# A language-model block on one core: the linear scan cut into runs of four tokens instead of single steps

## The reference

```
h  = relu(causal depthwise conv of width 2 over fake_quant(emb)[ids])     # 8 x 512 x 128
u  = layernorm(h)
# linear recurrence, 4 heads of 64 states, the same A (64x64) for every head:
x_t = x_(t-1) A + u_t B            # x_0 = init_states; written in the reference as an
                                   # associative scan over complex logarithms
x  = exp(log x - max over the head's 64 states + 2)       # = e^2 * x / max|x|
h  = h + x C + u D
n  = layernorm(h);  x_attn = (n*g + b) attn_w^T + attn_b + n
out = h + gelu(gelu(x_attn fc1^T + b1) fc2^T next^T + ...)  # 8 experts by position, hidden size 512
```

## Time and profile before

| | |
|---|---|
| median of three runs | 188.50 us (188.31 to 188.63) |
| profiled execution: own time | 188.72 us |
| its span, first to last instruction | 186.9 us |
| granted TensorE clock, mean | 0.997 |
| busy: PE, PEld, DVE, ACT, POOL | 169.2, 154.3, 135.4, 108.6, 106.5 us |

### The profile page before, as it was taken

The page is one execution under the profiler, slowest core; times in us unless marked ns, Lnnn a source line. Parts: engine busy times, 40 slices in busy tenths (PEclk is TensorE's granted clock), DMA queues, the critical chain, the costliest instruction groups (busy, mean ns, idle before and its releaser), DMA issues.

```text
span 186.9 us, 3886 instructions
## 1 busy us (share of the span) xinstructions
PE 169.2 (91%) x1327; PEld 154.3 (83%) x1327; DVE 135.4 (72%) x410; ACT 108.6 (58%) x289; POOL 106.5 (57%) x173
## 2 busy tenths in 40 slices
PE   0598899999999999799898899999999999997993
PEld 0187779999989999688587899999999999986882
DVE  1868974775444446667988999988889898628883
ACT  3026997745443334543445496785949778595782
POOL 3107664699900000323979678397896969789600
PEclk9999999999999999999999999999999999999998
DMA  5994000000000000000000000001010100101003
GB/s 147 321 438 182 5 0 5 2 0 0 4 0 0 4 0 0 2 4 0 0 0 0 4 0 2 4 2 56 0 60 0 53 7 2 58 4 58 24 32 112
DMA packets 2327, 7.42 MB, mean 40 GB/s; under 512 B 254, under 2 KB 892, under 8 KB 2052
## 3 DMA queue, kind: packets, MB, share of 16 engines
q1 hardware_dynamic: 2162, 7.05, 10.0%
q10 hardware_dynamic: 146, 0.13, 0.2%
HBM read 5.09 MB, written 2.10 MB: 38 GB/s over the span
## 4 chain that ended last, share of the span: by engine, by line
PE 53%; POOL 14%; DVE 12%; issue 9%; ACT 8%; DMA 2%; ACTq 0%; POOLq 0%; DVEq 0%
PE bank L966 8%; PE bank L969 7%; PE bank L1106 6%; POOL hid_p L437 6%; PE bank L1126 5%; PE bank L994 5%; PE bank L1053 4%; POOL rstd L467 3%; PE bank L943 3%; PE bank L899 2%; PE bank L920 2%; PE bank L983 2%; PE bank L1050 2%; ACT gel L560 2%; POOL X L449 2%
## 5 line engine op out<-in xcount | busy, mean ns | idle before, releaser
L437 POOL TENSOR_TENSOR hid_p<-hid_f,hid_p 128x256 fp32r<-128x256 f32 x52 | 37.5, 741 | 14.5 <-ACT hid_p L602 12.6
L600 ACT ACTIVATE hid_f<-bank,pa 128x256 f32<-128x256 f32 x64 | 30.8, 485 | 12.7 <-PE bank L1106 12.5
L1106 PE MATMUL bank<-xaT_p,fc_p 128*128 128x256 f32 x192 | 35.4, 296 | 1.7 <-ACT corr L577 0.7
L1126 PE MATMUL bank<-hid_p,out_hi 128*128 128x256 f32 x128 | 32.0, 286 | 0.3 <-POOL hid_p L437 0.3
L509 ACT ACTIVATE X<-bank 128x128 f32<-128x128 f32 x64 | 17.6, 278 | 22.7 <-PE bank L969 22.5
L1106 PEld LDWEIGHTS bank<-xaT_p,fc_p 128*128 128x128 f32 x192 | 26.7, 189 | 4.7 <-ACT hid_p L602 1.7
L966 PE MATMUL bank<-uT,pa 128*128 128x128 f32 x128 | 25.2, 281 | 0.1
L1126 PEld LDWEIGHTS bank<-hid_p,out_hi 128*128 128x128 f32 x128 | 23.3, 188 | 1.0 <-POOL hid_p L437 0.6
L602 ACT ACTIVATE hid_p<-bank,pa 128x256 fp32r<-128x256 f32 x48 | 23.5, 489 | 0.0
L969 PE MATMUL bank<-X,pa 128*128 128x128 f32 x120 | 23.2, 275 | 0.0
L444 POOL TENSOR_TENSOR E<-E,corr 128x248 f32<-128x248 f32 (+4 forms) x5 | 3.1, 626 | 32.0 <-ACT corr L585 32.0
(11 more groups left out here) (126 smaller groups left out, 369.8 us busy)
## 6 DMA issues: line engine op xcount, KB each, us to landing
fc_w<-in_fc SPq DMA_DIRECT2D x2, 2048.0 KB, 12.1
out<-res SPq DMA_DIRECT2D x7, 256.0 KB, 2.0
pb<-in_pack_b SPq DMA_DIRECT2D x1, 320.0 KB, 4.1
pa<-in_pack_a SPq DMA_DIRECT2D x1, 279.0 KB, 3.0
out<-res SPq DMA_DIRECT2D x2, 128.0 KB, 1.7
pc<-in_pack_c ACTq DMA_DIRECT2D x1, 128.5 KB, 3.0
pw<-in_pack_a SPq DMA_DIRECT2D x1, 64.0 KB, 3.8
emb_w<-in_emb SPq DMA_DIRECT2D x1, 62.5 KB
```

The lines of the kernel that those rows point to most:

```text
L437: nc.gpsimd.tensor_tensor(hid_p[1][:, half, c, :], hid_f[:, m % HID_SLOTS, :], hid_p[0][:, half, c, :].bitcast(F32), ALU.subtract).then_in ...
L600: full = nc.scalar.activation(hid_f[:, m % HID_SLOTS, :], src, ACT.Gelu, bias=bias)
L1106: last = mm(bank[5 + n % 2][:, 0:HALF], fc1_p[w][:, e * HID + c * P:e * HID + (c + 1) * P], xaT_p[m][:, b % 2, half, :], start=(k == 0), s ...
L1126: last = mm(out_bank(b, half)[:, half * HALF:(half + 1) * HALF], out_p[w][:, e, c * CH:(c + 1) * CH], hid_p[m][:, half, c, :], start=(c == ...
```

## The change

Group by group, the scan is done in four runs of four tokens in each chunk, all runs at once.

- `run_piece(g, n)`: the state at the end of each run from zero, as four accumulating matmuls over 512 columns (4 batches x 4 runs x 32 chunks): token `q` of the run times B A^(3-q). 8 such matmuls a group; ACT copies 512 columns a half (`copy_runs`). The products B A, B A^2, B A^3 (`late_b`) are two new `prepare` tasks, B^T comes with the first input pack.
- `ends(g)`: three matmuls over 248 columns (A^12, A^8, A^4) and one DVE add make the chunk ends from the run ends; the five doubling steps are as before, but their adds are DVE's in both groups (`ks_add`). They work in place 0 of `X`, which has 17 places now (`E` and `corr` are gone).
- `last_step(g, r)`: four steps of 256 columns with A^4, one after the other, each with a DVE add, give the state after each run.
- `state_input`, `state_step`: the three tokens inside all runs, per half one matmul with B and one with A over 512 columns, copied by ACT (`copy_state`).
- The powers of A that are kept are 1, 2, 3, 4, 8, 12, 16. `prepare` has 18 tasks as before, with 23 instead of 26 blocks of 128 columns.
- Placement: group 0's runs stand in embedding rounds 6 and 7, `ends`, the first doubling step and `fuse(0)`, `fuse(1)` in rounds 8 and 9 (ACT makes the high part now). After them come group 0's carries, with the first half of group 1's runs and `fuse(2)`, `fuse(3)` between, then group 0's states. `attn_g` and `centre` move behind the first doubling add on DVE. The second half of group 1's runs, its carries and its states fill the rounds -3, -2 and -1 by the new `PLAN`, and `fc1_part(0, 0)` waits for the last of them.
- POOL has no part in the scan any more. The embedding's tiles keep their own memory.

```diff
+POWERS = (1, 2, 3, 4, 8, 12, 16)
+RUN = 4
+RUNS = T // RUN
...
-        X = sb("X", [P, NG, NP * GB, T, NCH])
-        corr = sb("corr", [P, CORR_SLOTS, NP * GB, NCH])
-        E = sb("E", [P, NG, NP * GB, NCH])
+        X = sb("X", [P, NG, NP * GB, EXT, NCH])
...
+        PLAN = {
+            -3: (("run", "run"), (), ("run", "run"), (), ("fuse", "carry"), ("fuse", "carry"), ("fuse", "carry"), (), ()),
+            -2: (("carry",), ("input",), ("fuse", "input"), ("carry",), (), ("carry",), ("carry",), (), ("carry",)),
+            -1: (("carry",), (), ("carry", "step"), ("input", "step"), ("input", "step"), ("input",), ("step",),
+                 ("input", "step"), ("step",))}
+        ORDER = (0, 1, MIXER, 2, 3, 4, 5, 6, 7)
...
+                def copy_state(g, n):
+                    q, a = divmod(n, NP)
+                    act.wait_ge(state_done[g], n + 1)
+                    nc.scalar.activation(every_run(g, a, q + 1), scan_bank(a).rearrange("p (b r k) -> p b r k", b=GB, k=NCH),
+                                         ACT.Copy).then_inc(x_ready[g], 1)
...
+                for n in range(1 + LEVELS + RUNS):
+                    if n == 2:
+                        dve.wait_ge(ld_pb, 16)
+                        dve.wait_ge(ld_pa, 32)
+                        nc.vector.tensor_scalar(attn_g[:], pb[:, PB["attn"]], pa[:, PA["ln_g"]], None,
+                                                ALU.mult).then_inc(attn_g_ready, 1)
+                        nc.vector.tensor_scalar(centre[:], ident, -1.0 / CH, None, ALU.add).then_inc(centre_ready, 1)
+                    carry_add(0, n)
+                    if n in (3, 4, 8, 9):
+                        fused_lo((3, 4, 8, 9).index(n))
...
                 def scan_part(j, places):
                     for n in places:
                         for what, i in scan_work(j, n):
+                            if what == "carry":
+                                carry_add(1, i)
+                        for what, i in scan_work(j, n):
                             if what == "fuse":
                                 fused_lo(i)
...
+                def run_piece(g, n):
+                    a, q = divmod(n, RUN)
+                    if n == 0:
                         pe.wait_ge(uT_ready, GB * (g + 1))
...
+                    last = mm(scan_bank(a), b_then(a, RUN - 1 - q), u_runs(g, q), start=(q == 0), stop=(q == RUN - 1))
+                    if q == RUN - 1:
+                        last.then_inc(run_done[g], 1)
+
+                def ends(g):
+                    pe.wait_ge(run_ready[g], NP)
...
+                    for r in range(RUNS - 1):
+                        last = mm(carry_bank(g, NCH - 1), power(T - RUN * (r + 1)), X[:, g, :, RUN * (r + 1), 0:NCH - 1],
+                                  start=(r == 0), stop=(r == RUNS - 2))
+                    last.then_inc(ends_done[g], 1)
...
+                def last_step(g, r):
+                    if r == 0:
                         pe.wait_ge(ks_ready[g], LEVELS)
...
+                    mm(carry_bank(g, NCH), power(RUN), X[:, g, :, RUN * r, :], start=True, stop=True).then_inc(last_done[g], 1)
...
+                def state_input(g, n):
+                    q, a = divmod(n, NP)
+                    if q >= 1:
+                        pe.wait_ge(x_ready[g], n - 1)
...
+                    mm(scan_bank(a), b_then(a, 0), u_runs(g, q), start=True, stop=False)
+
+                def state_step(g, n):
+                    q, a = divmod(n, NP)
+                    if n == 0:
+                        pe.wait_ge(last_ready[g], RUNS - 1)
+                    mm(scan_bank(a), a1, every_run(g, a, q), start=False, stop=True).then_inc(state_done[g], 1)
...
-                    for i in embed_round_steps(b):
-                        scan_step(0, i)
+                    if b in (NB - 2, NB - 1):
+                        for q in range(RUN):
+                            run_piece(0, (b - (NB - 2)) * RUN + q)
+                    if b >= NB:
+                        carry_step(0, b - NB)
+                        fuse(b - NB)
                 prepare(N_PREP - 1)
-                for lv in range(LEVELS):
-                    ks_step(0, lv)
-                    scan_step(1, lv)
-                for i in range(T):
-                    second_pass(0, i)
-                    if (i + 1) % (T // WITH_SECOND) == 0:
-                        scan_step(1, LEVELS + i // (T // WITH_SECOND))
+
+                for n in range(RUN):
+                    carry_step(0, n + 2)
+                    run_piece(1, n)
+                carry_step(0, 6)
+                fuse(2)
+                carry_step(0, 7)
+                fuse(3)
+                carry_step(0, 8)
+                state_input(0, 0)
+                state_input(0, 1)
+                state_step(0, 0)
+                carry_step(0, 9)
+                state_step(0, 1)
+                for n in range(NP, NP * (RUN - 1)):
+                    state_input(0, n)
+                    state_step(0, n)
...
                         pe.wait_ge(xaT_ready, b + 1)
                         if b == 0:
                             pe.wait_ge(fc1_split, NE)
-                            pe.wait_ge(corr_ready, T)
+                            pe.wait_ge(x_ready[1], NP * (RUN - 1))
+                            pe.wait_ge(last_ready[1], RUNS)
                             pe.wait_ge(fused_lo_ready, NE)
```

More of the change, by code:

```diff
@@ L294, in embed_round_steps @@
-        def embed_round_steps(b):
-            return range(sum(G0_STEPS[:b]), sum(G0_STEPS[:b + 1]))
+        FUSED_FRONT = 4
+        MIXER = 8
+        PLAN = {
[3 more added lines that the diff above has]
+                 ("input", "step"), ("step",))}
@@ L303, in numbered @@
         def numbered(plan):
-            done, out = dict(step=LEVELS + WITH_SECOND, doubling=0, fuse=FUSED_FRONT, second=0), []
-            for names in plan:
-                place = []
-                for name in names:
-                    place.append((name, done[name]))
-                    done[name] += 1
-                out.append(place)
-            assert done == dict(step=T, doubling=LEVELS, fuse=NE, second=T)
+            done, out = dict(fuse=FUSED_FRONT, run=RUN, carry=0, input=0, step=0), {}
+            for j, places in plan.items():
+                for n in ORDER:
+                    out[j, n] = []
+                    for name in places[n]:
+                        out[j, n].append((name, done[name]))
+                        done[name] += 1
+            assert done == dict(fuse=NE, run=NP * RUN, carry=1 + LEVELS + RUNS, input=NP * (RUN - 1), step=NP * (RUN - 1))
             return out
@@ L540, in _, with scan_copies @@
                         last.then_inc(u_act_ready, 1)
-                    for i in embed_round_steps(b):
-                        copy_step(0, i)
+                    if b in (NB - 2, NB - 1):
+                        copy_runs(0, b - (NB - 2))
+                    if b >= NB:
+                        copy_fused(b - NB)
                 copy_out_prep(N_PREP - 1)
-                for lv in range(LEVELS):
-                    copy_step(1, lv)
-                for i in range(LEVELS, LEVELS + WITH_SECOND):
-                    copy_step(1, i)
+                copy_runs(1, 0)
+                for e in range(2, FUSED_FRONT):
+                    copy_fused(e)
+                for n in range(NP * (RUN - 1)):
+                    copy_state(0, n)
+                def scan_copies(j, n):
+                    for what, i in scan_work(j, n):
+                        if what == "fuse":
+                            copy_fused(i)
+                        if what == "run" and i % RUN == RUN - 1:
+                            copy_runs(1, i // RUN)
+                        if what == "step":
+                            copy_state(1, i)
                 def gelu_out(j):
@@ L567, in _ @@
                         if j < 0:
[L568 to L586 removed]
+                            scan_copies(j, n)
                         if n == LAG - 1 and j >= 1:
@@ L608, in _ @@
                                                      bias=bias).then_inc(last_hi_act, 1)
+                        if n == 1 and j < 0:
+                            scan_copies(j, MIXER)
                         b = j + 1
@@ L829, in _ @@
                     if j < 0:
[L830 removed]
+                        scan_part(j, [2, 3])
                     high_parts(j, range(2, 4))
@@ L1137, in fill @@
                             else:
-                                {"step": scan_step, "doubling": ks_step, "second": second_pass}[what](1, i)
+                                {"run": run_piece, "carry": carry_step, "input": state_input, "step": state_step}[what](1, i)
                     else:
@@ L1153, in _ @@
                         mixer_out(mixed, 1)
+                    if j < 0:
+                        fill(j, MIXER)
                     if 0 <= attended < NB:
```

301 lines of the change are left out of this document (133 added, 168 removed).

## The result

The changed kernel takes 187.12 us (median of four, 187.07 to 187.26) against 188.47 for the kernel before; the ratio on record is 0.9937, with a 95% interval of 0.9923 to 0.995. Forecast were 186.0 with a range from 184.8 to 187.9. So the direction was right, and of the 2.5 us forecast 1.35 came by these two medians and 1.2 by the ratio. Its profiled execution took 187.07 us, with a span of 185.3. Run again with twelve executions, the same kernel gave 187.09 against 188.21, ratio 0.9946 (0.9928 to 0.9964). Ratios leave out executions in a slower state of the chip, of which there was one here (e6, 198.21 us at a mean clock of 0.854).

What follows compares the result with a forecast made beforehand. Scan PE-bound with group 0, then passed between PE and DVE, ACT, POOL. 31.1 + (62.7 - 2.65) + 8.8 = 100.0 at the first expert matmul; `transpose_xa(1)` 2.55 earlier; median 186.0 us, range 184.8 to 187.9.

Steps and rivals of the forecast that it cites:

- half-gain rival: Strided 512-column matmuls and copies cost their upper bounds, or prepare(17) waits 1.7: about 187.2 us, chance 0.20.
- hand schedule: New order laid out with trace prices, last gather at 31.1 to first expert matmul at 100.0, waits 8.8 us.
- `transpose_u(7)` waits behind `u`: Rounds 8 and 9: PE waits 0.5 us for DVE's last u, at 40.05, a wait hidden before.
- the first expert matmul behind an ACT copy: End of round -1: PE waits 0.85 us for the last state copy, first expert matmul at 100.0.
- after `attn(0)` PE waits 2.4: Round -2: the second last step's matmul waits 2.4 us, as DVE's add stands behind xh(1) until 82.8.
- the forecast's 153.3: Forecast time from the last gather's start to the end of the span: 184.4 - 31.1 us.
- ten waits: PE's waits from the last gather to the first expert matmul, summed as 8.8 us against 8.0 before.
- 1.5 for 40 matmuls at 0.04: Extra cost of strided 512-column matmuls at their upper bound, a ground for about 187.2 us, chance 0.20.
- The blocked adds: Group 0's carry adds on DVE slowed by POOL's split until 51.4: about 190.5 us, chance 0.11.
- POOL's adds were off every path: Rounds -2 to 0: removing POOL's second-pass adds gives PE nothing but the earlier power.

Runs made afterwards that it cites:

- e6: Changed kernel with the first half of mixer_out(2) ahead of the first two fc1 parts in round 0: 186.20 us.
- e1: Changed kernel with two 512-column matmuls, results unread, in PE's wait of 1.9 us: 186.45 us.
- e12: The changed kernel once more, unedited, twelve executions: 187.09 us.
- e3: Changed kernel with POOL's fc1 split started only after DVE's last u: 186.28 us.
- e4: Changed kernel with attn_g and centre moved to embedding round 7 on DVE: 186.85 us.
- e10: Changed kernel with group 1's last-step adds on POOL and the two remaining waits filled with unused matmuls: 186.23 us.
- e13: As e11, but the filling matmuls write bank 2, which nobody has to leave: 184.28 us.
- e2: Changed kernel with fuse(7) moved between group 1's first last step and attn(0): 186.17 us.
- e5: Changed kernel with the edits of e2, e3 and e4, and fc1_part(0, 0)'s wait for x_ready[1] put last: 185.36 us.
- e11: As e9, with two waits filled by unused matmuls, the filler itself waiting for a low part: 185.23 us.
- e9: Changed kernel with the edits of e5 and e6, and group 1's last-step adds on POOL, waits unfilled: 184.13 us.
- e8: Changed kernel with group 1's four last-step adds on POOL after an ACT copy, waits unfilled: 186.41 us.

## Why the prediction was right or wrong

**The direction and the frame were right.** Matmuls go by columns: pairs of 512 columns start 0.86 apart in the trace after (0.853 taken), strided pieces and all, so the half-gain rival's first ground is gone; a copy of 512 columns over 4 x 4 pieces takes 0.60, as taken. The last gather (31.12 against 31.1), group 0's states, the mixer's start and the waits up to 82.88 stand within 0.5 us of the hand schedule. `transpose_u(7)` waits behind `u`, the first expert matmul behind an ACT copy, and from `transpose_xa(1)` to the end nothing changed.

**The step that failed** is the term "after `attn(0)` PE waits 2.4". As a wait it was right (79.92 + 0.89 to 82.88 is 2.1). But it was priced at its length alone, and the 2.2 us of PE work behind it at full clock. In the profiled execution, with 1.90 of that wait shown as idle, the granted clock then stood at 0.50 from 84.3 to 87.7. This wait had no match in the kernel before, where the longest idle time of PE between 31 and 105 us is the 0.68 of the earlier trace rows and whose clock was full in every slice but the last. Part of the price was hidden: the last step took 0.3 more and the mixer's half 1.2, 1.5 together, but the state step would have waited for DVE until 86.9 anyway, so 0.6 is left there. e1 gives the size, 0.67 in the medians and 0.7 in the profile; e12 shows the same 0.7 behind the last gather between two executions of one kernel.

That the idle time is the cause, and not something else that varies, rests on more than these profiles. Of the 32 executions in the ratios of kernels that keep the wait of 1.90 (the changed kernel both times, e3, e4, e6), 16 have a mean clock below 0.995 (the profiled one with its low stretch has 0.991). Where it is filled and the filler waits for nothing (e1, e10, e13), none of 13 has, and where it is cut to 1.01 (e2, e5), none of 9. No execution of the kernel before is below 0.996. With the clock held, the stretch from the last gather on is 153.5 against the forecast's 153.3. I had no rival in which PE's own waiting makes PE slower.

**What is left of the miss.** It is 1.1 us (187.12 - 186.0). For the profiled execution the forecast had 186.2 and 187.07 came, 0.9 more: 0.7 is the clock, and 0.2 is in the schedule. There PE went on 1.0 after the last state matmul where I had 0.85 (0.2 after the copy instead of 0.06, in front of five waits in a row), and 512 columns cost 0.858 (54.76 to 60.77 in seven steps). The prediction's own sums were a little short as well: by its prices the work falls by 2.55, not 2.65 (39.3 - 36.75), and its ten waits add up to 8.85, not 8.8. (Its 1.5 for 40 matmuls at 0.04 is 1.6.) The remaining 0.25 is the step from one execution to the median: I took 0.2 off, as the profiled execution before lay 0.2 above its median, but the profiled execution after lies 0.05 below its own.

**Where luck helped.** 187.12 lies inside the stated range, whose upper part stood there for the half-gain rival. That rival's mechanisms didn't come. The range held for reasons that the prediction doesn't contain.

**The rivals.** The blocked adds didn't come: the doubling adds took 0.40 and 0.39 and `fused_lo` 0.68 at 43.66 to 45.88, in the midst of the split:

```profile
43.66 0.40 DVE L705 TENSOR_TENSOR X<-X,bank 128x240 f32<-128x240 f32 x1 [0.99 <-PE bank L997]
44.89 0.39 DVE L705 TENSOR_TENSOR X<-X,bank 128x224 f32<-128x224 f32 x1 [0.83 <-PE bank L997]
45.20 0.68 DVE L717 TENSOR_TENSOR out_lo<-bank,out_hi 128x512 fp32r<-128x512 f32 x1
```

That is what the rule of the Trainium skill (SBUF — State Buffer, "Who interferes with whom") has for instructions with at most one input in SBUF, and the trace agrees now for the case itself. e3 shows the other side, the `u` pieces slowed by POOL's split, at 1.1 against 3.9. Half the gain came in size, but not by the mechanisms that I gave for it. That POOL's adds were off every path was wrong in what it left out: e10 gains 1.2 in the stage by giving four of them back to POOL, although each hop is 0.75 longer (82.38 to 84.35 from one last step to the next in e10, 82.99 to 84.21 in e1), since they no longer stand behind DVE's mixer pieces.

That the clock can fall behind a wait is in the trace after (0.50 at 84.3 to 87.7) and not in that of before; the row of this case that should have called for a rival is the forecast's own 2.4 us of idle PE. The Trainium skill (TensorE: Matmul & The Clock Gate, "Part 1: The HAM clock gate (the "warmup" mystery)") has the clock set by how busy TensorE has been recently, with two levels of 1.2 and 2.4 GHz, and says that at the start of one kernel the moment of its rise varies from run to run. The traces agree: 0.50 and 1.00 are the levels of these stretches, the second gather takes 1.39 in one execution of the changed kernel and 1.86 in another, and behind the same wait the one has the low stretch and the other doesn't.

## What to carry to other kernels

A schedule that opens a wait of a microsecond or two on PE, where there was none, should be priced with the low clock behind it as a case of its own: here 1.5 us of slower matmuls behind 1.9 us of waiting, 0.7 of it on the path, in half of the executions. Filling the wait with matmuls whose results nobody reads gave it back in e1; where the filler itself waited for DVE (e11), the kernel lost 1.1 against e9. And where a serial chain crosses an engine that is busy with blocks of 2 to 3 us, look at the place of its links in that engine's order first: here it weighed more (1.2 gained) than the length of a link (0.75 more each).

## What the runs showed of the hardware

**The clock behind a wait.** The same 1.90 us of idle PE was followed by a low stretch in one execution and not in another of the same kernel (mean clock 0.991 and 1.0). It also came behind waits of 0.75 and 1.27 with 0.7 us of work between (e8, two of six executions) and of 0.45 and 1.27 (e9, one of five), and not behind one of 1.01 (e2 and e5, none of nine). In the profile after it began 1.4 us after the wait of 1.90 had ended, with one more wait of 0.51 between, while PE was at work.

**What it goes with.** In the profiles the low stretch appeared in kernels whose last gather started at 30.95 to 31.37 us (the changed one, e4, e6, e8, e9), and among those with the wait of 1.90 it was absent in e3 and e12, at 31.53 and 31.61. That is a pattern over seven profiles, not a tested cause. An early start alone doesn't bring it: e1 and e5 started at 31.23 and 31.04, with the wait filled and with it cut to 1.01, and kept the clock. Since a late start costs 0.5 us and the low stretch 0.7, whole times of one kernel hide most of either. What fixes the moment stays open.
